# Cross-attention of a decoder layer: probabilities transposed so that the keys lie on the partitions, in four array tiles

## The reference

```
x = x + attn(layernorm(x), ...)
q, k, v = layernorm(x) @ Wq + bq, ctx @ Wk + bk, ctx @ Wv + bv     # 16 heads of 16
scores = einsum('blhd,bshd->bhls', q, k)                            # 512 queries x 64 keys
scores = where(triu(ones((512, 64)), k=1), -inf, scores)            # only queries 0..63 are masked
p = softmax(scores / sqrt(16), axis=-1)
x = x + einsum('bhls,bshd->blhd', p, v).reshape(8, 512, 256) @ Wo + bo
x = x + shared_expert(layernorm(x)) + top2_of_8_experts(layernorm(x))
```

## Time and profile before

| | us |
|---|---|
| median of 3 runs (lowest, highest) | 1039.25 (1034.06, 1040.99) |
| the profiled execution: its own time | 1037.41 |
| its span from first to last instruction | 1035.8 |
| mean granted TensorE clock | 0.968 of full speed |
| TensorE busy, VectorE busy | 959.8, 658.8 |
| ScalarE busy, GpSimd busy | 568.6, 358.8 |

### The profile page before, as it was taken

One profiled execution on the slowest core, in us unless ns is written; L12 is line 12 of the kernel. 1 busy time (PEld: TensorE's weight loads), 2 busy tenths in 40 slices (PEclk: granted clock), 3 DMA queues, 4 the chain that ended last, 5 costly groups with the idle time before them and its releaser, 6 DMA issues.

```text
span 1035.8 us, 21122 instructions
## 1 busy us (share of the span) xinstructions
PE 959.8 (93%) x7016; PEld 860.4 (83%) x7025; DVE 658.8 (64%) x1655; ACT 568.6 (55%) x1101; POOL 358.8 (35%) x297
## 2 busy tenths in 40 slices
PE   2989896899999977999999969999999999999995
PEld 2444795788888865888888969999999999999995
DVE  4888896688888746666665625656555655655452
ACT  2679652555555425445554435656565665666552
POOL 3651902133111106555555503333323342323322
PEclk9999898899999968999999989999999999999998
DMA  9200002000000021111111544342524252422322
GB/s 260 70 1 1 1 1 82 1 2 1 1 1 1 1 64 58 65 65 67 65 66 65 165 165 123 66 112 45 128 53 123 42 128 46 123 53 42 48 46 31
DMA packets 49025, 64.07 MB, mean 62 GB/s; under 512 B 10129, under 2 KB 42002, under 8 KB 48850
## 3 DMA queue, kind: packets, MB, share of 16 engines
q0 software_dynamic: 17504, 34.87, 14.2%
q1 hardware_dynamic: 31330, 27.52, 8.9%
q10 hardware_dynamic: 144, 1.05, 0.2%
HBM read 38.65 MB, written 24.77 MB: 61 GB/s over the span
## 4 chain that ended last, share of the span: by engine, by line
PE 55%; DMA 3%; DVE 1%; SPq 1%; issue 1%; ACT 0%; POOL 0%; DVEq 0%; POOLq 0%
PE PS L135 18%; PE PS L136 17%; PE PS L137 17%; PE PS L1416 2%; DMA routed_rows<-pads 1%; DMA bfc<-in_bfc 1%; DMA out_rows<-y,toki 1%; DMA xr<-routed_rows 1%; PE PS L1009 1%; SPq L989 1%; SPq L992 0%; PE PS L1034 0%; POOL out_rows L1490 0%; DVE hidl L141 0%; PE PS L1043 0%
## 5 line engine op out<-in xcount | busy, mean ns | idle before, releaser
L1490 POOL DMA_INDIRECT out_rows<-y,toki x70 | 124.0, 1771 | 281.8 <-DVE y L1529 271.1
L1462 ACT ACTIVATE hideh<-PS,be 128x256 fp32r<-128x256 f32 x280 | 139.7, 499 | 149.1 <-PE PS L137 149.1
L141 DVE TENSOR_TENSOR hidel<-act32e,hideh 128x256 fp32r<-128x256 f32 x280 | 117.8, 425 | 96.4 <-ACT act32e L1464 93.5
L135 PE MATMUL PS<-xTeh,wfch 128*128 128x256 f32 x560 | 159.6, 285 | 1.8 <-issue 1.1
L136 PE MATMUL PS<-xTel,wfch 128*128 128x256 f32 x560 | 158.4, 283 | 0.0
L137 PE MATMUL PS<-xTeh,wfcl 128*128 128x256 f32 x560 | 158.4, 283 | 0.0
L135 PE MATMUL PS<-wprh,hideh 128*128 128x256 f32 x560 | 157.9, 282 | 0.0
L136 PE MATMUL PS<-wprl,hideh 128*128 128x256 f32 x560 | 154.8, 277 | 0.0
L137 PE MATMUL PS<-wprh,hidel 128*128 128x256 f32 x560 | 154.8, 276 | 0.0
L1464 ACT ACTIVATE act32e<-PS,be 128x256 f32<-128x256 f32 x280 | 140.2, 501 | 8.0 <-DVE hidel L141 7.5
L135 PEld LDWEIGHTS PS<-xTeh,wfch 128*128 128x128 f32 x560 | 107.2, 191 | 3.4 <-issue 2.8
(11 more groups left out here) (236 smaller groups left out, 2297.9 us busy)
## 6 DMA issues: line engine op xcount, KB each, us to landing
xr<-routed_rows SPq DMA_DIRECT2D x36, 272.0 KB
fcraw<-in_Wfc POOLq DMA_DIRECT2D x8, 1024.0 KB, 6.2
prraw<-in_Wproj POOLq DMA_DIRECT2D x8, 1024.0 KB, 8.7
X<-in_x SPq DMA_DIRECT2D x8, 512.0 KB, 6.1
out_rows<-X SPq DMA_DIRECT2D x8, 512.0 KB, 3.0
routed_rows<-pads SPq DMA_DIRECT2D x8, 272.0 KB, 3.4
out_rows<-y,toki POOLq DMA_INDIRECT x70, 3.9
ctx<-in_ctxT SPq DMA_DIRECT2D x4, 256.0 KB
```

The source lines that it names most:

```text
L135: nc.tensor.matmul(out, wh, xh, start=first, stop=False)
L141: return eng.tensor_tensor(out, whole, high.bitcast(F32), ALU.subtract)
L1462: nc.scalar.activation(hid[0][:, j, :], PS[:, j % 4, 0:BLK], ACT.Gelu_apprx_tanh, bias=bias)
L1490: nc.gpsimd.indirect_dma_start(out=out, out_offset=bass.IndirectOffsetOnAxis(ap=toki[:, h:h + 1], axis=0), in_=y[:, h, :], in_offset=None, ...
```

## The change

In stage B the work of one batch is now issued as a whole, for all 512 queries. For each batch TensorE does:

- `row_scores`, four times: the old scores, as before with queries on the partitions, but only for the row maxima. One `tensor_reduce` of 1024 columns takes them; nothing is subtracted from these scores.
- `transpose_maxima`: the maxima of the 4 tiles, written twice side by side (`maxima_twice`), are transposed in 4 matmuls; ScalarE makes an fp32r copy (`maxima_high`) and VectorE one `scalar_tensor_tensor` of 512 columns (`maxima_split`) that keeps the high part in four rows and the low part in four others.
- `key_scores`, twice (m = 0, 1): the scores again, with the keys on the partitions: 4 fp32 matmuls of 32 rows and 512 columns in four row tiles of the array, one bank each; 4 fp32r matmuls with the matrix `sel` that subtract the maxima; 4 bf16 matmuls of 64 columns that add the causal mask. ScalarE's exponential (8 of 512 columns a batch) reads them from PSUM and writes `prT`, already transposed.
- `weigh_values`: 8 matmuls with 32 stationary value columns and 512 moving probability columns, in four column tiles, and 8 more like them with `onesbd` in place of the values, which give the sums of the probabilities, repeated for each of a head's 16 outputs.

`divide` is now, for each half m, a `reciprocal` of 512 columns on 128 partitions and a multiply of 512. The transposes of probabilities and of outputs are gone, the output projection has the same matmuls as before, two tiles at a time. `key_scores(b, 0)` waits for both divisions of batch b-1, since outputs and sums lie in the same four banks. GpSimd adds `bo` in four instructions of 256 columns. All loops are unrolled.

In stage C the SyncE list stores batches 0 to 5 first, then writes the padding and loads the first routed block, then stores batches 6 and 7. `load_weights(pool, 0)` comes behind the wait for `w_in`, and `load_weights(pool, 1)` behind a wait for the first routed block (`x_in`).

```diff
-                    def weigh_values(i, b): ...
+                    def key_scores(b, m):
+                        pe.wait_ge(mx_ready, b + 1)
+                        if m:
+                            pe.wait_ge(p_ready, 2 * NG * b + NG)
+                        elif b:
+                            pe.wait_ge(o_divided, KD * b)
+                        for j in range(NG):
+                            rows = slice(32 * j, 32 * j + 32)
+                            nc.tensor.matmul(PS[:, j, :], kbd[rows, b, m, j % 2 * P:(j % 2 + 1) * P],
+                                             qT[rows, b % 2, m, :], start=True, stop=False, skip_group_check=True)
+                        for j in range(NG):
+                            nc.tensor.matmul(PS[:, j, :], sel[rows, m, :], mxT[rows, :], start=False, stop=False, ...
+                        for j in range(NG):
+                            nc.tensor.matmul(PS[:, j, 0:S], ident16[:], causalT16[:], ...).then_inc(s_psum, 1)
+                    def weigh_values(b):
+                        pe.wait_ge(p_ready, 2 * NG * b + 2 * NG)
+                        for m in range(KD):
+                            for j in range(NG):
+                                nc.tensor.matmul(PS[32 * j:32 * j + 32, m, :], vbd[:, b, at:at + PW],
+                                                 prT[:, m, j, :], start=True, stop=True, skip_group_check=True)
+                            for j in range(NG):
+                                last = nc.tensor.matmul(PS[32 * j:32 * j + 32, 2 + m, :], onesbd[:], prT[:, m, j, :], ...
+                            last.then_inc(o_psum, 1)
...
+                    for b in range(B):                                   # TensorE
+                        key_scores(b, 0)
+                        row_scores(b + 1, 0)
+                        transpose_x(b + 2, 0)
+                        project_o(b - 1, 0)
+                        row_scores(b + 1, 1)
+                        key_scores(b, 1)
+                        row_scores(b + 1, 2)
+                        project_o(b - 1, 1)
+                        transpose_x(b + 2, 1)
+                        row_scores(b + 1, 3)
+                        weigh_values(b)
+                        transpose_maxima(b + 1)
+                        project_q(b + 2)
...
+                    def divide(b, m):                                    # VectorE
+                        dve.wait_ge(o_psum, KD * b + m + 1)
+                        link(nc.vector.reciprocal(oT[:, m, :], PS[:, 2 + m, :]))
+                        nc.vector.tensor_tensor(oT[:, m, :], PS[:, m, :], oT[:, m, :], ALU.mult).then_inc(o_divided, 1)
+                    for b in range(B):
+                        o_low(b - 1, 0); o_low(b - 1, 1)
+                        maxima(b + 1, 0)
+                        x_low(b + 2, 0)
+                        maxima(b + 1, 1)
+                        residual(b - 1, 0)
+                        stats_part(b + 3)
+                        maxima(b + 1, 2)
+                        x_low(b + 2, 1)
+                        residual(b - 1, 1)
+                        maxima(b + 1, 3); maxima_twice(b + 1)
+                        apply_part(b + 3, 0..3)
+                        divide(b, 0)
+                        maxima_split(b + 1)
+                        divide(b, 1)
...
+                    for b in range(B):                                   # ScalarE
+                        exps(b, 0); x_high(b + 2, 0)
+                        exps(b, 1); x_high(b + 2, 1)
+                        maxima_high(b + 1)
+                        evac_q(b + 2, 0); o_high(b, 0)
+                        evac_q(b + 2, 1); o_high(b, 1)
...
-                with sp.Fori(0, B - 1) as b:
+                for b in range(B - 2):
+                    store(b)
...
                 sp.dma_start(xr[:], rg[0].rearrange("p h c -> p h c")).then_inc(x_in, 16)
+                for b in range(B - 2, B):
+                    store(b)
...
-                load_weights(pool, 0)
                 pool_wait(pool, w_in, W_IN)
+                load_weights(pool, 0)
...
                 pool_wait(pool, e_low, 2)
+                pool_wait(pool, x_in, 16)
                 load_weights(pool, 1)
```

More of the change, by code:

```diff
@@ L580, in build, with pair @@
+            XB, YB, MB = 6, 7, 7
+            QB = (6, 4)
+            def pair(i):
+                return range(2 * i, 2 * i + 2)
             with nc.Block() as block:
@@ L615, in scores @@
                                 rows = slice(half * P // 2, (half + 1) * P // 2)
[L616 to L619, removed]
+                                at = PS[:, 4 + half, :].rearrange("p (i m n) -> p i m n", i=2, m=KD)[:, :, m, :]
@@ L620, in scores @@
+                                last = nc.tensor.matmul(
+                                    at, qT[rows, b % 2, m, t * P:(t + 1) * P],
+                                    kbd[rows, b, m, :].rearrange("p (i n) -> p i n", i=2),
+                                    start=m == 0, stop=t > 0 and m == KD - 1, skip_group_check=True)
                                 if t and m == KD - 1:
-                                    last.then_inc(s_psum, 1)
+                                    last.then_inc(n_psum, 1)
@@ L622, in scores @@
                         if t == 0:
                             for half in range(2):
[L624 to L645, removed]
@@ L665, in step @@
[L665 to L680, removed]
@@ L682, in _, with transpose_maxima @@
-                    for t in range(TB):
-                        transpose_x(t, t, (6, 7, 5, 4)[t])
+                                nc.tensor.matmul(PS[:, 4 + half, :], ident16[:], causal16[:], start=False, stop=True,
+                                                 skip_group_check=True).then_inc(n_psum, 1)
+                    def transpose_maxima(b):
+                        pe.wait_ge(mx_twice, b + 1)
+                        if b > 1:
+                            pe.wait_ge(x2_ready, 2 * (b - 1))
+                        for t in range(TB):
+                            last = nc.tensor.transpose(PS[:, MB, t * P:(t + 1) * P], mxpad[:, t, :], ident[:])
+                        last.then_inc(mxT_psum, 1)
@@ new lines, in project_o @@
+                    def project_o(b, i):
+                        u = 2 * b + i
+                        pe.wait_ge(oT_ready, KD * b + KD)
+                        if u:
+                            pe.wait_ge(x2_ready, u)
+                        for t in pair(i):
+                            for k in range(KD):
+                                last = product(PS[:, YB, t % 2 * D:(t % 2 + 1) * D],
+                                               [x[:, k, t * P:(t + 1) * P] for x in oTp],
+                                               [w[:, k, :] for w in wop], k == 0, k == KD - 1)
+                        last.then_inc(y_psum, 1)
@@ L684, in _ @@
+                    for i in range(2):
+                        transpose_x(0, i)
                     pe.wait_ge(w_split, 1)
@@ L686, in _ @@
                     for t in range(TB):
[L687 to L693, removed]
-                        step(B - 1, t, following=False)
-                    for t in range(3):
-                        step(B, t, scored=False, following=False, lag2=t < 2)
+                        row_scores(0, t)
@@ new lines, in _ @@
+                    low(nc.vector, wqp[1][:], wq[:], wqp[0][:]).then_inc(w_split, 1)
+                    for i in range(2):
+                        x_low(0, i)
+                    stats_part(1)
+                    dve.wait_ge(w_high, 2)
+                    low(nc.vector, wop[1][:], wo[:], wop[0][:]).then_inc(w_split, 1)
+                    dve.wait_ge(t_in, 32)
+                    nc.vector.tensor_copy(sel[:], selraw[:])
+                    nc.vector.tensor_copy(causalT16[:], causalT[:]).then_inc(consts_ready, 1)
@@ L904, in _ @@
                             norm_apply(0)
-                    for t in range(TB):
-                        step(B, t, scored=False, following=False, lag3=t < 3)
-                    dve.wait_ge(x2_ready, N // P)
+                        divide(b, 0)
+                        if ahead:
+                            maxima_split(b + 1)
+                        divide(b, 1)
+                    for m in range(KD):
+                        o_low(B - 1, m)
+                    for i in range(2):
+                        residual(B - 1, i)
@@ L1595 @@
     small[:, 40:48] = -0.5
+    small[:, 20] = np.where(np.arange(P) % 32 // 4, -1.0, 0.0)
+    sel = np.zeros((P, 2, 2, S), np.float32)
+    for r in range(P):
+        if r % 32 < 8:
+            sel[r, r % 4 // 2, r % 2] = -1.0
+    sel = sel.reshape(P, -1)
     causal = np.where(np.arange(S)[None, :] > np.arange(P)[:, None], np.float32(-1e30), np.float32(0))
@@ L1612 @@
         "small": small, "causal": np.tile(causal, (1, HH)),
+        "causalT": np.tile(np.where(np.arange(S)[:, None] > np.arange(S)[None, :], np.float32(-1e30), np.float32(0)), (2, 1)),
```

(1 more changed line is left out.)

407 lines of the change are left out of this document (202 added, 205 removed).

## The result

| | before | after |
|---|---|---|
| median of 4 runs each (lowest, highest), us | 1036.95 (1034.06, 1040.99) | 1062.28 (1060.70, 1062.84) |
| ratio, 95% interval | | 1.0224, 1.0182 to 1.0266 |
| span of the profiled execution, mean granted clock | 1035.8, 0.968 | 1060.8, 0.943 |
| stage B's end (stage C's first DMA issue) | 380.08 | 416.49 |
| from there to the end of the span | 655.7 | 644.3 |

The changed kernel is slower by 2.2%. The two medians of the table divide to 1.0244, which lies inside the interval of the ratio. The time lies inside the range given (1010 to 1070) and 18 us above the number given (1044), but outside the forecast's own range (1030 to 1058). By place, in the profiled executions: stage B +36.4 us, stage C -11.4, sum +25.0, the difference of the spans.

A forecast was written before the change was run, and what follows sets the result against it. TensorE bounds the attention before; after, VectorE's two reciprocals make TensorE wait, 26.0 us a batch with the lower clock. 1037.4 + 18.0 (stage B) - 11.2 (stage C) = 1044 us, own range 1030 to 1058, overall 1010 to 1070.

The forecast's parts named there:

- rival (c): Stage B's reciprocal repeats a step eight times per number, 8.3 ns a number, 4.4 us each: total 1063; chance 0.12.
- TensorE's sum, 18.8 us: Stage B: TensorE's work per batch after the change, with row and column tiles taken as fully parallel, is 18.8 us.
- Rival (d): Stage B's value matmuls: column tiles don't run at once, values take 13.9 us, a batch 32.3: total 1094; chance 0.07.
- The reciprocal, 3.25 us: `divide` in stage B: one VectorE reciprocal of 512 columns takes 3.25 us, within 1.9 to 3.6, twice a batch.
- (a): Stage B's reciprocal costs 1.9 to 2.3 us, the clock falls seldom, a batch takes 22.5: total 1018; chance 0.25.
- (b): Stage B's reciprocal costs 1 ns a number, TensorE sets the pace at 20 us a batch: total 992; chance 0.06.
- The order of a batch, 24.7 us with 5.3 us of wait: Stage B, engine lists side by side: a batch takes 24.7 us, TensorE waiting 5.3 for the banks that the divisions hold.
- I charge 1.3 (0 to 2): Stage B: lower granted clock after TensorE's wait adds 1.3 us a batch, 0 to 2, making 26.0.
- Batches 0 to 4: 5 x 26.0 - 1: Stage B's first five batches take 26.0 us each, less 1 because the first has no residual.
- The first `key_scores` at 193.0: Start of stage B: after first scores near 176.65, 9.6 us of row scores and 6.8 more, key scores start at 193.0.
- Batch 7 and the tail 27.0: End of stage B: last batch with its tail takes 27.0 us, 17.3 to the last division, the rest at half clock.
- Stage C, -11.2: Stage C's moved stores and weight loads save 11.2 us, bounds 5 and 13, mostly TensorE's wait for the first routed block.

The follow-up runs named there:

- the last experiment: Changed kernel with the sums' inverse on ScalarE, GpSimd's low halves later, and its first bias also waiting for batch 1's normalisations: 1006.12 us, ratio 0.9681 to before.

## Why the prediction was right and wrong

The 18 us by which it fell short lie all in stage B. The sign and the mechanism of a regular batch came out, the size did not: 1044 would have been a change below the 1% that the prediction called measurable, and 1062 lies outside the forecast's own range of 1030 to 1058. It is inside the range given because that was drawn for the rivals too, and it falls on the 1063 of rival (c), which the trace rules out: by the time alone one would have picked the wrong rival. By the prediction's own steps:

- **TensorE's sum, 18.8 us: right.** The copy in the reciprocal's place shows 18.6 busy in a batch of 19.6, with row and column tiles fully parallel. Rival (d), column tiles one after another, is ruled out.
- **The reciprocal, 3.25 us: right, 3.35 measured.** The upper of the two rows of 16 numbers was the better guide to 512. Rivals (a) and (b) are out. So is (c), whose eight steps a number would have been 4.4 us. The Trainium skill's sentence on the repeat count of 8 ("VectorE: DVE Perf Modes", section "Walkthrough: the 8-slice pipeline in each mode") gives no time, and the 8.3 ns a number that rival (c) made of it don't hold here: 6.5 were measured.
- **The order of a batch, 24.7 us with 5.3 us of wait: right.** The wait was 5.19, and 24.3 and 24.6 us is what the batch takes with the clock held up.
- **"I charge 1.3 (0 to 2)" for the clock: mis-sized.** In the batches 1 and 2 it was 1.8 and 2.3, near and beyond its upper bound of 2. Batch 0 was charged the same 1.3 though no wait stands ahead of it: it took 23.3 us with and without the matmuls in the waits. By chance the two errors cancel: the first three batches were 23.3, 26.1 and 26.9 against 25, 26 and 26.
- **"Batches 0 to 4: 5 x 26.0 - 1": failed for two of the five.** Batches 3 and 4 took 62.1 us together, 10.1 more than the 52 charged. The step left out what GpSimd does beside VectorE: with the change GpSimd takes `rstds(b + 1)` before `add_bo(b)`, so that the low half that follows stands just ahead of the next batch's normalisations instead of behind those of its own. Timeline of the kernel before, where the low half lies between two normalisations and beside none:

```profile
242.07 0.41 DVE L807 TENSOR_SCALAR hn<-X,mv,rstd 128x256 f32 x1
...
244.96 4.61 POOL L141 TENSOR_TENSOR wpsl<-prraw,wpsh 128x2048 fp32r<-128x2048 f32 x1
...
251.05 0.41 DVE L807 TENSOR_SCALAR hn<-X,mv,rstd 128x256 f32 x1 [2.04 <-POOL rstd L122]
```

The prediction counted the four normalisations at the 1.35 us that they take alone; what it held of GpSimd was that the long bias instruction is "gone from VectorE's way". The Trainium skill has the collision, on "SBUF — State Buffer", section "Who interferes with whom": `tensor_scalar` can run in a mode that takes the pair of ports that VectorE shares with GpSimd, and then whichever of the two issues first holds the pair for its whole instruction and the other is fully blocked. The rows agree with the blocking: 5.69 us beside 4.59 of GpSimd, 1.37 once the wait is there. That the normalisations ran in such a mode no run shows.
- **"The first `key_scores` at 193.0": failed, 199.2.** The first bias is the same collision, beside GpSimd's four additions (2.94 us instead of 1.38); with the low clock that follows it, 4.1 us counted from the normalisations, as the last experiment shows. Another 1.6 are the kernel after's own execution (23.5 us from there, against 21.9 or 22.0 in the four others). The last 0.5 are within what two executions differ by.
- **"Batch 7 and the tail 27.0": mis-sized, 28.6.** It took 29.1 to stage C's first issue, of which 0.5 lie behind the stage's end, as before (379.6 and 380.08). The excess is ahead of the last division, which ended 19.6 us into the batch where the prediction had 17.3. The mean granted clock of the whole was 0.68; no experiment took this apart, and the cause stays open.
- **Stage C, -11.2: right, -11.4.** With its edits alone it is -10.1.

Start +6.2, batches 0 to 2 -0.6, batches 3 and 4 +10.1, batches 5 and 6 +1.2, tail +1.6 make 18.4 us (rounded terms add to 18.5). The predicted end of 397.6 and the 0.5 to the first issue make 398.1, and with 18.4 that is the measured 416.5.

Not tried: column tiles one after another, a doubled reciprocal, and the attention's change without stage C's edits; the last is known only from differences, 32 to 35 us.

## What to carry to other kernels

When a change trades many small operations for a few wide ones, look first for the one whose cost grows with each number: here 16 numbers a row became 512, and two reciprocals a batch undid what 40 transposes less gave. An engine that is relieved gains nothing while it waits for its banks, as TensorE did here; lay the lists side by side up to the wait that ends last, and put the slow step on the engine that idles there. Whenever a long GpSimd instruction moves, look at what VectorE reads and writes in SBUF beside it in its new place.

## What the runs showed of the hardware

- A reciprocal of 128x512 from PSUM took 3.35 us in every batch, beside GpSimd's low half too (3.34); four normalisations from SBUF to SBUF took 5.69 instead of 1.37 beside the same instruction. What differs between them is the source and the operation; which of the two decides wasn't taken apart.
- ScalarE's two logarithms and two exponentials of 512 columns (0.60 us each, and two table loads of 1.28 us a batch) gave the sums' inverse sooner for the whole than VectorE's reciprocal of 3.35 us a half: a batch of 20.5 us instead of 26.9.
- With a wait of 5.2 us of TensorE ahead, the granted clock averaged 0.63 over the next 7.4 us; 20 bf16 matmuls whose result nobody reads, put in the wait, kept it at 1.00 in the batches 1 to 3 and made the kernel 14 us faster.
